# Starting GpSimd's scatter into the list by source after the last count instead of before the counting

## The reference

```python
edge_index = jnp.stack([src, dst])
h = relu(layernorm(x)); x = x + L0(h, src, dst)             # three rounds of a degree-scaled filter
h = relu(layernorm(x)); x = x + L1(h, edge_index, ...)      # graph attention, 8 heads
h = relu(layernorm(x)); x = x + L2(h, edge_index, type, w)  # relational convolution, three rounds
h = relu(layernorm(x)); x = x + L3(h, edge_attr, ...)       # attention with edge terms

# L0, the layer that this case is about
deg = segment_sum(ones(E), dst, N)
dinv = clip(deg, 1) ** -0.5
h = THETA[0] * feat
for k in 1, 2, 3:
    agg = segment_sum((feat * dinv)[src], dst, N)
    feat = feat - agg * dinv
    h = h + THETA[k] * feat
```

## Time and profile before

| what | us |
|---|---|
| median of 3 runs (lowest to highest) | 7069.73 (7066.88 to 7076.96) |
| the profiled execution | 7046.59 |
| its span in the trace | 7044.6 |
| PE busy over the span | 4200.1 (60%) |
| DVE busy | 3150.8 (45%) |
| POOL busy | 3222.8 (46%) |

### The profile page before, as it was taken

The page is one execution under the profiler, slowest core; times in us unless marked ns, Lnnn a source line. Parts: engine busy times, 40 slices in busy tenths (PEclk is TensorE's granted clock), DMA queues, the critical chain, the costliest instruction groups (busy, mean ns, idle before and its releaser), DMA issues. The chain is left out here.

```text
span 7044.6 us, 85720 instructions
## 1 busy us (share of the span) xinstructions
PE 4200.1 (60%) x18026; PEld 2739.5 (39%) x18027; DVE 3150.8 (45%) x8308; ACT 856.9 (12%) x2517; POOL 3222.8 (46%) x3301
## 2 busy tenths in 40 slices
PE   6820111167799677777775658888788743333433
PEld 6800000022399544434434544444444432333322
DVE  6910011177698455555556771221121254444445
ACT  2200000011110021212111001010010012222221
POOL 0077777700000166666661004646646446666663
PEclk6555555588899777788787989898898955555555
DMA  4300000013367466666663546676575542223332
GB/s 122 88 17 11 11 2 2 11 49 90 121 246 274 149 183 173 184 172 179 174 181 92 146 121 239 220 238 219 206 253 202 182 126 71 70 73 73 74 71 58
DMA packets 564874, 910.99 MB, mean 129 GB/s; under 512 B 100563, under 2 KB 402664, under 8 KB 526004
## 3 DMA queue, kind: packets, MB, share of 16 engines
q1 hardware_dynamic: 459630, 742.44, 32.6%
q0 software_dynamic: 105024, 166.00, 10.5%
HBM read 677.34 MB, written 230.78 MB: 129 GB/s over the span
## 5 line engine op out<-in xcount | busy, mean ns | idle before, releaser
L2030 POOL DMA_INDIRECT l_edges_by_src<-l_by_src,src_i x816 | 786.5, 964 | 1495.5 <-POOLq L1764 1002.5
L3020 POOL DMA_INDIRECT l_gathered<-l_table,l_st x816 | 776.5, 952 | 1003.6 <-issue 833.6
L402 POOL DMA_INDIRECT by_src<-src_rec,src_pos x784 | 815.6, 1040 | 546.7 <-DVEq L315 290.4
L2030 POOL DMA_INDIRECT l_edges_by_src<-l_q,src_i x816 | 778.3, 954 | 563.4 <-DVE l_scores L3160 241.6
L3089 PE MATMUL psum<-l_blocks,l_rows 128*128 128x512 f32 (+1 forms) x2016 | 881.8, 583 | 75.7 <-issue 73.0
L2124 PE MATMUL psum<-l_rows,l_edges_hot_t 128*128 x1632 | 420.7, 433 | 792.7 <-DVE l_scores L3160 637.0
L1929 PE MATMUL psum<-pair_hot_weight,pair_hot_dst 128*128 128x512 f32 x1200 | 731.7, 754 | 176.5 <-DVE pair_hot_dst L1919 109.3
L2124 PEld LDWEIGHTS psum<-l_rows,l_edges_hot_t 128*128 128x128 f32 x1632 | 359.0, 313 | 861.9 <-issue 861.8
L1163 PE MATMUL psum<-hot_block,hot_low_src 128*128 128x400 bf16 x1136 | 338.1, 420 | 591.6 <-issue 295.9
L3048 DVE TENSOR_SCALAR l_hot<-iota,l_loc,l_weight 128x128 f32<-128x128 f32 x816 | 225.7, 357 | 1024.9 <-DMA pair_blocks<-pair_block 236.0
L1135 DVE TENSOR_SCALAR hot_block<-block_iota,visit_key 128x400 bf16<-128x400 f16 x1136 | 284.9, 322 | 812.9 <-remote 526.7
(11 more groups left out here) (561 smaller groups left out, 5223.6 us busy)
## 6 DMA issues: line engine op xcount, KB each, us to landing
l_blocks<-pair_blocks SPq DMA_DIRECT2D x216, 1024.0 KB
l_counts<-counts SPq DMA_DIRECT2D x67, 1600.0 KB, 7.1
pair_blocks<-pair_block SPq DMA_DIRECT2D x75, 1024.0 KB
l_edges_loc<-loc_by_tile SPq DMA_DIRECT2D x416, 128.0 KB
l_rows<-l_edges_by_src SPq DMA_DIRECT2D x204, 256.0 KB
l_sum_rows<-l_rows SPq DMA_DIRECT2D x204, 256.0 KB
counts<-count_rows SPq DMA_DIRECT2D x25, 1600.0 KB, 7.1
attr_space<-in_edge_attr SPq DMA_DIRECT2D x14, 1568.0 KB
```

Of the source, the lines that this page charges most:

```text
L402: pool.indirect_dma_start(table, bass.IndirectOffsetOnAxis(ap=pos[:, e:e + 1], axis=0), rec[:, e, :], None).then_inc(s_out[g % R], 16)
L2030: pool.indirect_dma_start(a[:, r, g, :], None, table_src, bass.IndirectOffsetOnAxis(ap=k.src_i[:, n * G + g:n * G + g + 1], axis=0))\
L3020: pool.indirect_dma_start(sent[:, p, g, :], None, by_type, bass.IndirectOffsetOnAxis(ap=st[:, p, g:g + 1], axis=0))\
```

## The change

GpSimd gets one more wait ahead of its scatter: for the last of the 200 closing matmuls of the counting (W * PER_WINDOW = 25 * 8). Nothing is removed, no other engine's list is touched, and the instructions of GpSimd keep their order.

```diff
@@ -1238,6 +1238,7 @@
         counts.gpsimd(pool)
         pool.wait_ge(k.s_list_pads, 16 * CH)
         pool.wait_ge(s_pos, 1)
+        pool.wait_ge(counts.s_sum, W * PER_WINDOW)
         send_edges(pool, s_sent, rec, pos, k.list_src)
```

## The result

| on the chip of the first measurement | us (median, lowest to highest) |
|---|---|
| before | 7068.31 (7058.81 to 7076.96, 4 runs) |
| changed | 7158.03 (7154.21 to 7163.49, 4 runs) |
| ratio | 1.0127, 95% interval 1.0113 to 1.0142 |

The change makes the kernel 89.7 us slower there. The forecast was +62, 7130, with a range of +17 to +165. The profiled execution of the changed kernel took 7161.33 us, its span is 7159.4.

What follows compares the result with a forecast made beforehand. TensorE's instruction stream was taken to bound the block, at 1.40 us per instruction beside the scatter. Counting to 963, scatter 1010, recovery 27 put the filter at 2000 instead of 1938: +62, about 7130 us; range +17 to +165, 7087 to 7235.

Steps and rivals of the forecast that it cites:

- Counting without the toll: Counting, no longer beside the scatter: half turns every 3.0 us, last count at 963 instead of 1886.9, 924 us earlier.
- the toll: TensorE's stream beside the scatter: each instruction takes 1.40 us, whatever it does, as long as the scatter lasts.
- the preparation: Unrolled matmuls ahead of the counting loop: the remaining 53 at 0.34 us take 18 us, done at 404.
- the turns: 14 turns between preparation and counting loop: 1.12 us each on TensorE plus some 0.3, 20 us, done at 424.
- Scatter: GpSimd's 784 indirect DMAs, starting at 963: 1.29 us each, 1010 us (985 to 1097), ending at 1973.
- Degrees under the toll: Degree sums beside the scatter: 824 TensorE instructions, 48.6 us before, would take 1007 us, from 965 to 1972.
- the free passage: Start of the degrees beside the scatter: the first 136 TensorE instructions pass within 44 us, before 1.40 us each applies.
- Filter: Stage after the degrees: counted as started at 2000, 27 us behind the scatter, instead of 1937.6; its 436.4 us stay.
- The first rival: Degrees and filter pay no toll, done at 1448; block ends with the scatter: -401, about 6670 us; chance 0.16, in part or whole.
- The third: Block end: quicker counting, scatter at 1.256 us per DMA and shorter recovery leave no difference, within 0.2%; chance 0.08.
- The second: Counting is slow by itself and keeps its end at 1886.9: +523, about 7590 us; chance 0.03, shared with a longer scatter.

Runs made afterwards that it cites:

- 512-byte rows: Kernel before with the scatter's 784 DMAs writing 128 rows of 512 bytes, not 16-byte records; no edges in the list: 7565.16 us against 7116.32 (chip 11).
- gathers: Kernel before with 784 gathers of 128 16-byte records in place of the scatter, list holding pads alone: 7528.82 us on chip 1, 6209.21 on chip 9.
- The kernel with bursts: Kernel before with 25 small GpSimd memsets behind every 21 scatter DMAs: 5881.37 us against 5619.98, ratio 1.0448 (chip 13).
- pauses: Kernel before with four small GpSimd memsets behind each scatter DMA: 6971.12 us against 7064.52 (chip 1); 6306.96 against 5619.98 (chip 13); 6327.3 (chip 7).

## Why the prediction was right, and where it wasn't

**Counting without the toll: right.** The loop began at 407.3 (I had 424) and half turns came every 3.0 us. The last L1163 started at 940.3, 963 forecast. 17 of the 23 us are the preparation, whose last matmul started at 394.6 in place of 404, and the turns, which took 11 us (394.8 to 405.9) in place of 20.

**Scatter: mis-sized, +60.** 1070 us (943 to 2013), 1010 forecast, inside the bounds of 985 to 1097. I took 1.29 us per DMA because degree sums are unrolled like the preparation. That reading of the earlier trace rows was wrong. The spacing does not follow TensorE's code but the place in the scatter. The changed kernel, GpSimd alone, with degree sums in both stretches:
```profile
1012.00:1200.00 188.00, 142.65 (x149) 0.50 0.03 2
1200.00:1600.00 400.00, 309.49 (x287) 0.50 0.02 2
```
188/149 is 1.26 us, 400/287 is 1.39. In each of the four traces with the toll (before, changed, 512-byte rows, gathers) some 185 to 210 DMAs stand 1.26 us apart and the rest 1.40 on average: in the kernel before the step comes near 600 us, in the changed one near 1205. The first 200 take 253 us in both, the other 583 take 817 and 816. So the whole length, 1071 us in the earlier trace rows, could have been carried over as it stood. Why the step comes there is open; on the chips without the toll, DMAs beside resting engines keep 1.26 to the end.

**Degrees under the toll: the pace right, the length mis-sized, +64.** From the last count at 943 until VectorE takes up the last sum (L1069) at 2014.3 they last 1071 us, 1007 forecast. The VectorE steps L1056, one for each window, are 44.80 us apart from 1017.5 to 2003.1, and 32 TensorE instructions at 1.40 are 44.8. What I had wrong is the free passage. By TensorE's records it is as large as I allowed, 171 instructions in the first 69 us. But these records run ahead of what the other engines see. One window's last matmul and the VectorE step that waits for it, in the kernel before:
```profile
1930.24 0.28 PE L1121 MATMUL psum<-tile_values,one_row 1*128 1x128 bf16 x2
1930.56 0.35 DVE L1056 TENSOR_SCALAR_CACHE_REDUCE degree_junk<-psum,degree_levels 128x128 f32<-128x128 f32 x1 [0.68 <-PE psum L1121]
```
and the last window's in the changed kernel, with what follows:
```profile
1914.91 0.26 PE L1121 MATMUL psum<-tile_values,one_row 1*128 1x128 bf16 x1 [2.55 <-issue]
2003.11 0.35 DVE L1056 TENSOR_SCALAR_CACHE_REDUCE degree_junk<-psum,degree_levels 128x128 f32<-128x128 f32 x1 [44.37 <-remote]
2003.88 0.62 PE L1124 MATMUL psum<-edges_up_to,degrees_down 128*128 128x25 f32 x2 [88.71 <-issue]
2004.32 0.60 PE L1125 MATMUL psum<-edges_up_to,degrees_down 128*128 128x24 f32 x2
2014.31 0.18 DVE L1069 TENSOR_TENSOR deg<-edges_up_to,psum 128x25 f32<-128x25 f32 x1 [10.55 <-issue]
```
In the kernel before, VectorE follows the matmul by 0.2 to 1.8 us in every window. Under the toll it follows by 88.2 us from the fifth window on, which is 63 steps of 1.40. Counted by what VectorE sees, 16 + 3 x 32 = 112 instructions are through at 1017.5, 59 more than 1.40 us each would give and not some 105, and the missing 46 at 1.40 are the 64 us. So a start in TensorE's records doesn't say that the instruction's result is out; where the instruction stands in between, the trace doesn't show.

**Filter: counted as begun 27 us behind the scatter; right, at 23.** Its first matmul starts at 2016.1 (1938.2 before), right behind the degrees, and its last at 2464.4 (2366.7): 77.9 us later begun, and 448.3 us long where it was 428.5. That is the 97.7 us. In its first 29 us from 2013 TensorE has 51 matmuls, then 3760 in 430 us.

The sum on record had 963 + 1010 + 27; it came out as 943 + 1070 + 23. So -20, +60 and -4 go on top of +62: about +98, and +97.7 was measured in the profile. Two errors of opposite sign hid each other in part; that the forecast came as near as it did is partly luck. Scatter and degrees end within 2 us of each other, in the forecast as in the trace, so the trace doesn't say which of the two the filter would have waited for if one had been shorter. Another way to see it: all work up to the last count takes 600 us clean (342.6 to 943), of which 443 were left when the scatter of before was over the earlier trace rows. So that scatter hid 157 us of work. The scatter of the change hides the degrees' 49. The first rival, degrees and filter that pay nothing, did not come on the chip of the first measurement. The third, no difference, needed a scatter of 985 us. The second, counting that is slow by itself, is refuted by counting that ran clean as soon as the scatter stood behind it.

**What the prediction said of the toll was too narrow, in three ways.** First, it took the toll for a property of the program. It goes with the chip, or the occasion, as well (no chip was drawn on two occasions): the first measurement, chip 11 and chip 1 have it, chips 7, 9 and 13 don't, and on chip 9, the only one of these where it ran, the change costs 420 us, for a reason that isn't in the prediction at all (the scatter starts 602 us later and ends the block). My range does not hold there. Second, "it goes with the scatter" is shown only for DMAs that GpSimd issues back to back. With other GpSimd work between them it is gone on a chip that has it. Third, I read 22.3 us per half turn as 16 instructions at 1.40. As a pace that stands, but the loop's records don't show 16 steps. In the gathers' trace on chip 1 eight pairs of weight load and matmul stand 1.40 us apart, most of them, and then 12.6 us pass until the next pair:
```profile
1030.20 0.49 PE L1177 MATMUL psum<-hot_block,hot_low_src 128*128 128x400 bf16 x1 [10.02 <-issue]
1039.99 0.49 PE L1177 MATMUL psum<-hot_block,hot_low_src 128*128 128x400 bf16 x1 [0.91 <-issue]
1052.59 0.49 PE L1177 MATMUL psum<-hot_block,hot_low_src 128*128 128x400 bf16 x1 [12.11 <-issue]
```
The first and second row are the first and last of a half turn, the third begins the next, 22.4 us behind the first. In the kernel before, eight matmuls are recorded within 2.85 us from 1365.39 on, and VectorE, which waits until they have read its blocks, goes on at 1406.26, 38 us behind their recorded end. That is the lead of TensorE's records again. The loop also has a register instruction for each matmul (1136 of them at L1163); a toll of 1.40 us on these too would make 24 steps, 33.6 us a half turn, where 22.3 was measured.

**Still open.** What in the row of indirect DMAs holds TensorE, and why on some chips only. One candidate can be put aside by the trace: that TensorE's instructions come too slowly from memory. In the filter of the kernel before, 7620 TensorE instructions go with 30 packets of 16 KB on this queue of instructions, 254 to a packet:
```profile
q8 instruction: 30, 0.49, 0.5%
```
From 600 to 1410 us, in the turns and the loop, the same queue brings nothing, and the toll is there. Nor is it density alone: in the later layers the gathers stand 1.25 us apart too, in bursts of some 20 with 5 us between, and TensorE runs at 0.18 us an instruction, on a chip with the toll. In the scatter the toll set in some 44 us, 34 DMAs, after the start. So the toll may need a row of DMAs that goes on unbroken for longer than those bursts. The kernel with bursts would test that; it ran on a chip without the toll only. How short a pause suffices is open with it. What a cheaper pause would save can only be estimated. The bursts have 25 memsets for 21 DMAs, and L153 stood at 1859.9 with them on chip 13. If they ended the toll as the pauses did, the block would end near there on a chip with the toll, some 520 us before the kernel before, 2381.2. That wasn't run.

## What to carry to other kernels

When an engine slows down beside work that it shares nothing with, look at what the other engine issues and at what pace. Then run the same program on another chip before making that pace a rule. Where a stretch has been measured whole, carry over its whole length: the 1071 us of this scatter came back as 1070, and the rate read from a part of it was off by 60. Moving an overlap only moves the price: here 784 DMAs hid 157 us of clean work before and 49 after, and the difference is about what the change cost. Where the price is not charged, a background transfer belongs as early as possible, since its end is the block's.

## What the runs showed of the hardware

- One program, 7064 to 7116 us on three chips (or occasions) and 5620 to 5644 on three others, though executions on any one agree within 1%. The block holds 761 us of the difference (L153 at 2381.2 and 1619.9), the later layers the rest.
- Indirect DMAs with 128 rows each stand 1.25 to 1.26 us apart beside resting engines, scatter or gather (chip 9). On the chips with the toll the first 185 to 210 of the 784 stand 1.26 apart and the rest 1.40, whether they write 16 or 512 bytes a row.
- Under the toll other engines see a matmul's result up to 88 us after its recorded start (0.2 to 2 us without it).
- Beside VectorE's counting, on a chip without the toll, the scatter's stand 1.87 us apart on average and 3.0 in the slowest stretch; gathers 1.48 on average.
- With memsets between the DMAs, one single DMA is recorded as 99 to 113 us long, at the filter's start, on chips of both kinds:
```profile
1025.70 111.50 POOL L404 DMA_INDIRECT by_src<-src_rec,src_pos  x1 [0.28 <-POOL pool_rest L407]
```
That row is from the kernel with pauses on chip 1. The gathers on chip 9 have one of 65 us. I have no cause for it. TensorE and VectorE were at their busiest then.
